# A transformer block on one core: where the first chunk of the MLP is projected, normalised and turned

## The reference, cut to what matters

```
# B = 2, N = 2048 tokens, H = 576, 16 heads of 36, MLP = 2304, all float32
mod = swish(c) @ w_mod + b_mod          # six vectors a batch: shift, scale, gate, twice
xn  = ln(x) * (1 + sc_msa) + sh_msa
q, k, v = split(xn @ w_qkv + b_qkv);  q = ln(q, g_q);  k = ln(k, g_k)    # per head
o   = softmax(q k^T / 6) v
x   = x + g_msa * (o @ w_proj + b_proj)
xn2 = ln(x) * (1 + sc_mlp) + sh_mlp
x   = x + g_mlp * (gelu_tanh(xn2 @ w1 + b1) @ w2 + b2)
```

## Time and profile before

| what | value |
|---|---|
| median of 3 runs | 2894.0 us (2893.54 to 2894.77) |
| the profiled execution | 2893.01 us, span 2891.1 us |
| PE busy | 2787.1 us, 96% |
| DVE, ACT, POOL busy | 1996.3, 1524.2, 689.4 us |
| last attention group | about 1709 to 1884 us of the span |
| between it and the first MLP product | 1883.94 to 1912.03 us |

### The profile page before, as it was taken

How to read it: one execution, slowest core, us unless ns; L and a number is a source line. 1 busy time by engine, 2 the same in 40 slices (tenths; PEclk the granted TensorE clock), 3 DMA queues, 4 the chain that set the end, 5 groups by cost and what they waited for, 6 DMA issues and landing times.

```text
span 2891.1 us, 43560 instructions
## 1 busy us (share of the span) xinstructions
PE 2787.1 (96%) x14764; PEld 1438.4 (50%) x14764; DVE 1996.3 (69%) x2677; ACT 1524.2 (53%) x2218; POOL 689.4 (24%) x502
## 2 busy tenths in 40 slices
PE   5579999999999999999999999989999999999999
PEld 1334444444444444444444444447575665757666
DVE  5668888888888888888888899954435344353421
ACT  2457777778887777777777777821211112121110
POOL 0143346642223333333333321010000000000000
PEclk9689999999999999999999999989999999999999
DMA  5142222222211122222223224140211202011000
GB/s 173 66 80 52 52 63 78 81 61 51 55 46 32 29 47 60 72 71 71 69 75 78 70 64 144 37 145 7 88 39 50 75 14 88 23 66 66 24 17 17
DMA packets 231121, 180.26 MB, mean 62 GB/s; under 512 B 148923, under 2 KB 176001, under 8 KB 230860
## 3 DMA queue, kind: packets, MB, share of 16 engines
q1 hardware_dynamic: 230694, 178.35, 22.4%
q10 hardware_dynamic: 296, 0.07, 0.0%
HBM read 98.77 MB, written 46.04 MB: 50 GB/s over the span
## 4 chain that ended last, share of the span: by engine, by line
PE 93%; DVE 2%; issue 1%; ACT 1%; POOL 1%; DVEq 0%; ACTq 0%; POOLq 0%
PE at_ps L1434 18%; PE at_ps L895 16%; PE at_ps L892 15%; PE at_ps L883 15%; PE at_ps L1458 15%; PE at_ps L911 10%; PE at_ps L949 1%; DVE at_plo L742 1%; PE at_ps L1424 1%; ACT at_aff L660 0%; PE at_ps L922 0%; ACT at_p L634 0%; POOL at_ssq L551 0%; PE at_ps L933 0%; ACT at_xy L608 0%
## 5 line engine op out<-in xcount | busy, mean ns | idle before, releaser
L742 DVE TENSOR_TENSOR at_plo<-at_p 128x1024 fp32r<-128x1024 f32 x1024 | 1267.0, 1258 | 199.2 <-ACT at_p L634 192.1
L634 ACT ACTIVATE at_p<-at_ps 128x1024 f32<-128x1024 f32 x1024 | 1047.0, 1025 | 406.9 <-PE at_ps L883 406.9
L895 PE MATMUL at_ps<-at_plo,at_vr 128*37 128x512 f32 x2048 | 1072.1, 591 | 0.0
L892 PE MATMUL at_ps<-at_p,at_v 128*73 128x512 bf16 x2048 | 796.3, 389 | 0.7 <-DVE at_plo L742 0.7
L1434 PE MATMUL at_ps<-ml_w2s,ml_hid 128*128 128x288 f16 x3456 | 428.1, 286 | 2.0 <-issue 2.0
L1458 PE MATMUL at_ps<-ml_xhi,ml_w 128*128 128x512 f16 x1296 | 399.2, 381 | 3.5 <-issue 3.5
L1434 PEld LDWEIGHTS at_ps<-ml_w2s,ml_hid 128*128 128x128 f16 x3456 | 338.0, 98 | 86.9 <-issue 2.5
L892 PEld LDWEIGHTS at_ps<-at_p,at_v 128*73 128x73 f16 x2048 | 232.7, 114 | 241.0 <-DVE at_plo L742 2.3
L537 POOL TENSOR_TENSOR at_tssq<-at_tssq,head_eps 128x8 f32<-128x8 f32 x112 | 124.0, 1107 | 924.3 <-DVE at_tssq L712 924.3
L895 PEld LDWEIGHTS at_ps<-at_plo,at_vr 128*37 128x37 f32 x2048 | 233.5, 114 | 222.5
L911 PE MATMUL at_ps<-wq,at_xhi 128*128 128x432 f16 x1008 | 297.6, 350 | 19.1 <-DVE at_txc L716 18.5
(11 more groups left out here) (150 smaller groups left out, 2313.6 us busy)
## 6 DMA issues: line engine op xcount, KB each, us to landing
head_sums<-at_oT SPq DMA_DIRECT2D x256, 72.0 KB
ml_held<-head_sums SPq DMA_DIRECT2D x64, 256.0 KB
at_xy<-in_L_cond_w SPq DMA_DIRECT2D x34, 288.0 KB
w_halves<-wq SPq DMA_DIRECT2D x68, 144.0 KB
at_xy<-in_x SPq DMA_DIRECT2D x32, 288.0 KB, 2.8
ml_x<-in_x SPq DMA_DIRECT2D x8, 1152.0 KB, 5.6
out<-ml_x SPq DMA_DIRECT2D x7, 1152.0 KB, 4.5
wm<-in_L_cond_w_mod SPq DMA_DIRECT2D x6, 1152.0 KB, 13.9
```

Source lines behind the costliest of these rows:

```text
L634: act.activation(p[:, s % NP, :], ps[:, 2 * (s % 2):2 * (s % 2) + 2, :].rearrange("p a n -> p (a n)"), ACT.Exp).then_inc(exp_done, 1)
L742: nc.vector.tensor_tensor(plo[:, s % NP, :], p[:, s % NP, :], high, ALU.subtract).then_inc(plo_ready, 1)
L892: nc.tensor.matmul(acc[0:VW, bass.ds((U % 2) * CH, CH)], v16[:, h % 2, 2 * s + a, 0:VW], high, start=(s == 0 and a == 0), stop=False, skip ...
L895: last = nc.tensor.matmul(acc[0:RW, bass.ds((U % 2) * CH, CH)], vr[:, h % 2, 2 * s + a, 0:RW], plo[:, s % NP, a * CH:(a + 1) * CH], start= ...
```

## The change

In the last attention group the PE loop over units is written out, and the work of chunk 0 gets places inside it.

- The five blocks of sums follow each other one unit apart (units 4 to 8, formerly two); the addition of the two parts moves from DVE to POOL; DVE multiplies in step 3, ACT casts in step 5, DVE subtracts in step 6.
- The projection of token tile i is made in unit 9+i: three pairs of matmuls in each of steps 2 and 3, two in each of steps 4 to 7, in banks 6 and 7. DVE multiplies by the gate in step 7; in unit 10+i it adds (step 0), makes moments (steps 1, 2) and the normal form (step 5).
- In unit 14 PE turns the five blocks (steps 0, 1, 3, 4, 6), ACT scales, shifts and casts (steps 1, 2, 4, 5, 7), DVE subtracts (steps 2, 3, 5, 6 and step 0 of unit 15).
- SP loads the gates' rows in unit 1 and w1 in unit 8. POOL's power of chunk 0 comes in units 10 to 13, and its addition of the second bias to the residual rows (L1242) may begin once the last normal form is made.
- After the group `up(0)` comes at once. SP's order after the group, and the places of chunk 1's additions and casts inside `up(0)`, are the same. DVE's reciprocal of the second denominators now comes before anything else that DVE does there.

```diff
+                if G == GROUPS - 1:
+                    rest.gpsimd_early(pool, u)
...
+                    if G == GROUPS - 1 and fixed:
+                        rest.tensor_early(pe, u, s)
...
+                    for u in range(UNITS):
+                        attend(G, u // NCH, u % NCH)
+                    continue
...
-    SUMS_AT, ADD_IN, MULTIPLY_IN, HIGH_IN, LOW_IN = ({u0 + 2 * k: k for k in range(KC)} for u0 in (4, 5, 6, 7, 7))
+    SUMS_AT, ADD_IN, MULTIPLY_IN, HIGH_IN, LOW_IN = ({u0 + k: k for k in range(KC)} for u0 in (3, 4, 4, 4, 4))
+    PROJECT_IN = {9 + i: i for i in range(TPC)}
+    PROJECT_AT = (None, None, (0, 3), (3, 6), (6, 8), (8, 10), (10, 12), (12, 14))
+    NORMAL_IN = {10 + i: i for i in range(TPC)}
+    TURN_IN = 14
+    TURN_AT, AFFINE_AT, LOW_X_AT = ({s: k for k, s in enumerate(at)} for at in ((0, 1, 3, 4, 6), (1, 2, 4, 5, 7), (2, 3, 5, 6)))
...
+    def early_pair(self):
+        return self.ps[:, 6:8, 0:HALF]
...
+            sp.dma_start(self.gates[:, :, :, :].rearrange("p b v n -> p (b v n)"), bcast(self.gates_dram, 0, P)).then_inc(self.gates_loaded, 16)
...
-        if u == 5:
+        if u == 8:
             self.load_w1(sp)
-        if u == 7:
-            sp.dma_start(self.gates[:, :, :, :].rearrange("p b v n -> p (b v n)"), bcast(self.gates_dram, 0, P)).then_inc(self.gates_loaded, 16)
...
+    def gpsimd_early(self, pool, u):
+        if u in self.ADD_IN:
+            k = self.ADD_IN[u]
+            pool.wait_ge(self.held_loaded[k % 2], 16 * self.so_far[k])
+            pool.tensor_tensor(self.total(k), self.total(k), self.slot[:, k % 2, 1, :], ALU.add).then_inc(self.added, 1)
+        if u in self.NORMAL_IN:
+            i = self.NORMAL_IN[u]
+            pool.wait_ge(self.first_mv, i + 1)
+            pool.tensor_tensor(self.rstd[:, 0, i:i + 1], self.mv[:, i, 1:2], self.keep.eps[:, 0:1], ALU.add).then_inc(self.first_var, 1)
+            pool.wait_ge(self.first_var, i + 1)
+            pool.tensor_tensor(self.rstd[:, 1, i:i + 1], self.rstd[:, 0, i:i + 1], self.keep.power[:, 0:1], ALU.pow).then_inc(self.first_rstd, 1)
...
-        if u in self.ADD_IN and s == 2:
-            self.add_o(dve, 0, self.ADD_IN[u])
-        if u in self.MULTIPLY_IN and s == 2:
+        if u in self.MULTIPLY_IN and s == 3:
             self.multiply_o(dve, 0, self.MULTIPLY_IN[u])
-        if u in self.LOW_IN and s == 5:
+        if u in self.LOW_IN and s == 6:
             self.low_o(dve, 0, self.LOW_IN[u])
+        if u == 9 and s == 1:
+            self.nc.vector.memset(self.xlo[KT:P, KF, :], 0.0).then_inc(self.xlo_zero, 1)
+            dve.wait_ge(self.gates_loaded, 16)
+            dve.wait_ge(self.x_loaded, 16)
+        if u in self.PROJECT_IN and s == 7:
+            i = self.PROJECT_IN[u]
+            self.gate_part(dve, i, i, self.early_pair, 0, 0)
+        if u in self.NORMAL_IN:
+            i = self.NORMAL_IN[u]
+            if s == 0:
+                self.add_part(dve, 0, i, i, self.x1_ready)
+            if s == 1:
+                dve.wait_ge(self.x1_ready, i + 1)
+                for h in range(2):
+                    last = self.nc.vector.bn_stats(self.stats[:, i, h, :], self.x1[:, i, h * HALF:(h + 1) * HALF])
+                last.then_inc(self.first_stats, 1)
+            if s == 2:
+                dve.wait_ge(self.first_stats, i + 1)
+                self.nc.vector.bn_aggr(self.mv[:, i, :], self.stats[:, i, :, :].rearrange("p a b -> p (a b)")).then_inc(self.first_mv, 1)
+            if s == 5:
+                dve.wait_ge(self.first_rstd, i + 1)
+                row = self.x1[:, i, :]
+                for c0, c1, at in ((0, H, 0), (KF * P, H, H)):
+                    last = self.nc.vector.tensor_scalar(self.tok[:, i, at:at + c1 - c0], row[:, c0:c1], self.mv[:, i, 0:1],
+                                                        self.rstd[:, 1, i:i + 1], ALU.subtract, ALU.mult)
+                if i == TPC - 1:
+                    last.then_inc(self.y_ready, 1)
+        if u == self.TURN_IN and s in self.LOW_X_AT:
+            self.low_x(dve, 0, self.LOW_X_AT[s])
+        if u == self.TURN_IN + 1 and s == 0:
+            self.low_x(dve, 0, KF)
...
-        nc.vector.memset(self.xlo[KT:P, KF, :], 0.0).then_inc(self.xlo_zero, 1)
-        dve.wait_ge(self.gates_loaded, 16)
-        first_project()
...
+    def tensor_early(self, pe, u, s):
+        if u in self.PROJECT_IN and self.PROJECT_AT[s]:
+            i, (n0, n1) = self.PROJECT_IN[u], self.PROJECT_AT[s]
+            ops = list(split_products(self.ohi, self.olo, self.wp, slice(i * P, (i + 1) * P), slice(0, H)))
+            if n0 == 0:
+                if i == 0:
+                    pe.wait_ge(self.olo_ready, KC)
+                    pe.wait_ge(self.wp_loaded, 16 * 7)
+                    pe.wait_ge(self.ends.t_yn, self.TILES + 1)
+                else:
+                    pe.wait_ge(self.pair_taken, i)
+            for n in range(n0, n1):
+                l, w = ops[n]
+                for half in range(2):
+                    last = self.nc.tensor.matmul(self.early_pair[:, half, :], l, w[:, half * HALF:(half + 1) * HALF],
+                                                 start=(n == 0), stop=(n == len(ops) - 1))
+            if n1 == len(ops):
+                last.then_inc(self.pair_ready, 1)
+        if u == self.TURN_IN and s in self.TURN_AT:
+            if s == 0:
+                pe.wait_ge(self.pair_taken, TPC)
+            self.turn_y(pe, 0, (self.TURN_AT[s],))
...
-                if J == 0 and i == 0:
-                    pe.wait_ge(self.wp_loaded, 16 * 7)
-                    pe.wait_ge(ends.exp_done, self.UNITS_DONE * STEPS + 2)
-                if J == 0 and i == 1:
+                if J == 1 and i == 1:
...
+                    pe.wait_ge(ends.exp_done, self.UNITS_DONE * STEPS + 2)
...
-        project(0, 0)
-        turn_y(0, range(KC))
```

More of the change, by code:

```diff
@@ L1227, in gpsimd @@
         for J in range(self.CHUNKS):
[L1228 to L1234, removed]
+            if J:
                 pool.wait_ge(self.mv_ready, J)
@@ L1247, in high_o, with affine @@
         act.copy(self.ohi[:, k, :], self.total(k)).then_inc(self.ohi_ready, 1)
+    def affine(self, act, J, k):
+        n = J * KC + k
+        act.wait_ge(self.xt_ready, n + 1)
+        act.wait_ge(self.xlo_ready, n + (0 if k else 1))
+        col = lambda v: self.keep.cols[:, J // NCH, v, k:k + 1]
+        act.activation(self.aff[:, k % 2, :], self.tr_bank(k), ACT.Identity, bias=col(2), scale=col(3)).then_inc(self.aff_ready, 1)
+        act.wait_ge(self.aff_ready, n + 1)
+        act.copy(self.xhi[:, k, :], self.aff[:, k % 2, :]).then_inc(self.xhi_ready, 1)
     def scalar_early(self, act, u, s):
-        if u in self.HIGH_IN and s == 0:
+        if u in self.HIGH_IN and s == 5:
             self.high_o(act, 0, self.HIGH_IN[u])
+        if u == self.TURN_IN and s in self.AFFINE_AT:
+            self.affine(act, 0, self.AFFINE_AT[s])
     def scalar(self, act):
[L1254 to L1262, removed]
         def gelu(J, f):
@@ L1269, in gelu @@
                            scale=1.0 / WS).then_inc(self.gelu_done, 1)
-        affine(0)
         act.wait_ge(self.b1_loaded, 16)
@@ L1279, in scalar @@
             if more:
-                affine(J + 1)
+                for k in range(KC):
+                    self.affine(act, J + 1, k)
     def add_o(self, dve, J, k):
@@ new lines, in vector_early, with gate_part @@
+        if u == self.TURN_IN and s in self.LOW_X_AT:
+            self.low_x(dve, 0, self.LOW_X_AT[s])
+        if u == self.TURN_IN + 1 and s == 0:
+            self.low_x(dve, 0, KF)
+    def gate_part(self, dve, i, r, pair, b, v):
+        dve.wait_ge(self.pair_ready, r + 1)
+        gate = self.gates[:, b, v, :].rearrange("p (h n) -> p h n", h=2)
+        self.nc.vector.tensor_tensor(self.part[:, i % 2, :].rearrange("p (h n) -> p h n", h=2), pair, gate, ALU.mult).then_inc(self.pair_taken, 1)
@@ new lines, in add_part, with low_x @@
+    def add_part(self, dve, J, i, r, after):
+        row = self.x1[:, (J % 2) * TPC + i, :]
+        dve.wait_ge(self.pair_taken, r + 1)
+        self.nc.vector.tensor_tensor(row, row, self.part[:, i % 2, :], ALU.add).then_inc(after, 1)
+    def low_x(self, dve, J, k):
+        rows = P if k < KF else KT
+        dve.wait_ge(self.xhi_ready, J * KC + k + 1)
+        self.nc.vector.tensor_tensor(self.xlo[0:rows, k, :], self.aff[0:rows, k % 2, :], self.xhi[0:rows, k, :], ALU.subtract).then_inc(self.xlo_ready, 1)
@@ L1316, in residual @@
         def residual(J, i, r, v, after):
[L1318 to L1323, removed]
+            self.gate_part(dve, i, r, self.pair(i), J // NCH, v)
+            self.add_part(dve, J, i, r, after)
         def project(J, r0):
@@ L1347, in project @@
             last.then_inc(self.y_ready, 1)
[L1349 to L1378, removed]
         def hidden(J, f):
@@ L1392, in down @@
                 if turn:
[L1393 to L1397 removed]
+                    for k in self.WITH_DOWN[i]:
```

(13 more changed lines are left out.)

8 lines of the change are left out of this document (5 added, 3 removed).

## The result

The kernel became slower by 0.32%: 2902.79 us (median of 7, 2900.54 to 2904.12) against 2893.54 (7 runs, 2891.69 to 2894.77) of the kernel before; the ratio is 1.0032, 95% interval 1.0021 to 1.0044. The forecast was 2901, range 2889 to 2907. The profiled execution took 2903.68 us, its span is 2901.8.

A forecast was written before the change was run, and what follows sets the result against it. PE was taken to bound attention. From attention's former end to the second projection, 16.1 + 3.6 + 15.1 + 16.5 + 39.3 + 2.7 = 93.3 us against 85.2; 8.1 us on the profiled 2893.0 gave 2901, range 2889 to 2907.

The forecast's parts named there:

- work moved into the group: Last attention group on PE: 112 projection matmuls at 13.8 us and 20 turns at 2.3 us, together 16.1 us.
- block 0 landed: First block of chunk 1's sums arrives 28.6 us after attention's end on PE, 6.6 us after being asked for.
- PE's stall: In `up(0)`: PE stops at 15.1 us after attention and goes on at 31.6, a new stall of 16.5 us.
- What bounds it, and the gap's worth: PE bounds attention; the gap before `up(0)`, which starts 28.1 us after attention, is the target; half clock costs 2.7 us.
- What is late next: Inside `up(0)`: chunk 1's sums, queued behind w2, come only 2.6 us earlier than before, so DVE, ACT and PE wait.
- five tiles of credit: In `up(0)`: with three gelus done PE can finish five feature tiles, until 15.1 us after attention, then stops.
- rows 9: Profile row: a small store issued behind w1 in unit 5 was waited for 10.5 us; used to expect queueing behind w2.
- Stalls in attention: Last attention group: 1.0 us in units 4 to 8, 0.6 in 13 and 14, 2.0 from ACT; sum 3.6 us.
- A: Rival after attention: the reciprocals' store overtakes w2, so PE stops only 4.9 us; 2889.5 us, chance 0.13.
- B: Rival in `up(0)`: the sums land before DVE asks, no new wait; 11.1 us less, 2882 us, chance 0.08.
- C: Rival: attention stretches; POOL blocks DVE for whole instructions, or ACT's unit 14 bursts cost twice; 2907 us, chance 0.11.
- D: Rival in `up(0)`: the wait comes, but PE's clock doesn't fall or the cast doesn't block gelu; 2898.5 us, chance 0.10.

The follow-up runs named there:

- the four runs on the order: The changed kernel with SP's order of w2, the reciprocals' store and chunk 1's sums altered in four ways: 2902.73, 2889.07, 2895.59 and 2904.24 us.
- e3_ask_later: The changed kernel, with DVE adding chunk 1's sums behind feature tiles 3, 6, 9, 12, 14 instead of 1, 4, 7, 10, 13: 2895.78 us.
- e1_sums_first: The changed kernel, with SP issuing the reciprocals' store and blocks 0 and 1 of chunk 1's sums before all of w2: 2902.73 us.
- e7_gates_after: `e5_halves_later`, with POOL's addition of the second bias to the residual rows held back until attention has ended: 2883.82 us.
- e11_half_w2: The changed kernel, with half of w2 ahead of the reciprocals' store and the other half behind block 4 of chunk 1's sums: 2895.59 us.
- e5_halves_later: `e3_ask_later`, with SP issuing blocks 0 and 1 before w2's first half and its second half behind block 4: 2884.54 us.
- e10_add_on_dve: `e7_gates_after`, with the five early additions of the sums moved from POOL back to DVE: 2882.51 us.

## Why the prediction was right

| step | forecast | measured |
|---|---|---|
| work moved into the group | 16.1 | 16.0 (units 9 to 12: 14.35 for 10.9; turns 0.44 a block) |
| stalls there | 3.6 | 4.9 |
| SP asks for the sums, after the last attention sum | 22 | 21.05 |
| block 0 landed | 28.6 | 29.0 |
| PE's stall | 16.5 | 16.46 |
| attention to second projection | 73.6 | 73.4 (1906.46 to 1979.84) |
| total (measured: 20.9 - 11.9) | +8.1 | +9.0 |

- *What bounds it, and the gap's worth.* Right: the gap of 28.1 us went, and the half clock came back behind the new stall.
- *What is late next.* Right in each link: the queue behind w2 (the four runs on the order), DVE's place (`e3_ask_later`, which moved ACT's cast along with it), ACT's cast in front of the fourth gelu (20.52 us of wait there), five tiles of credit. Two sizes were off and cancelled: the store landed 1 us earlier, and block 0 took 7.9 us from the first request and not 6.6.
- *The base.* I added 8.1 to the profiled execution and not to the median of 2894.0, which would have given 2902.1.
- *The control of rows 9.* A small store that waited 10.5 us behind w1 was the one row that told the chain's order, and it held: 14.05 us behind w2 here, about 1.7 in `e1_sums_first` with nothing ahead (issued at 1913.12, the sums asked for at 1914.85).
- *Stalls in attention.* The sum was near, 3.6 for 4.9, partly by luck, for the split was wrong. I gave ACT 2.0 in unit 14; PE waited 0.4 us for it in the kernel after, and the stall left in `e7_gates_after` is 1.3. I gave DVE 1.6; the other 3.6 or so are its. The mis-sized term is what POOL costs DVE. I multiplied POOL's lengths where DVE was idle by the 0.26 of the earlier trace rows, whose POOL lengths are those beside DVE: 3.1 us. The nine additions took 25.9 us for the 11.9 I had put, and lengthened DVE's instructions by 9.5. The Trainium skill ("SBUF — State Buffer", "Who interferes with whom") says that a DVE instruction with two SBUF inputs and a GpSimd instruction that reads SBUF exclude each other whole. The trace agrees with it: each of the nine additions held up one such DVE instruction, by most of an addition's length, and the 9.5 us are nearer to its 11.9 than to my 3.1.
- *Rivals.* A and B are refuted by the kernel after: the store landed behind w2, and DVE waited 20.00 us. Of C, most came on DVE (6.4 us more than I had put, where C has 8.8), but little reached PE, 1.3 where C has 6. D did not happen: the clock fell as forecast, and the cast held the gelu back.

## What to carry to other kernels

When work moves ahead into a free stretch, list what its successor asks for, and when each answer starts: a chain that starts at a fixed event (here the end of attention) doesn't move with it. A large load without a near reader belongs behind the small ones that have one, and the issuing engine's own time in a full queue counts as well. Read how long an operation takes from rows where its neighbour is busy, and look at single instructions beside it: a mean over a group hides that a few are held up whole.

## What the runs showed of the hardware

- An issue of a DMA can block the issuing engine: x took 0.44 us to issue in one run and 7.36 behind w2, w2 itself 3.60 and 9.04. The reciprocals' store took 7.26 us to issue behind all of w2, and 0.34 behind half of it (`e11_half_w2`).
- The clock may fall after a very short stop. Before the last chunk's product with w2 PE stands 2.0 us. In nine of the twelve traces the clock then stays full, in three it falls to 0.50 (1.2 GHz), and the end of the kernel is 1.67 us longer. Windows of 3 us there, in `e5_halves_later` and `e7_gates_after`:

```profile
2825.00:2828.00 3.00, 3.00 (x15) 1.82 (x13) 0.00 (x0) 0.00 (x0) 0.00 (x0) 0.50 0.00 0
```

```profile
2825.00:2828.00 3.00, 3.00 (x27) 2.38 (x26) 0.00 (x0) 0.00 (x0) 0.00 (x0) 1.00 0.00 0
```

From the second projection to the end all kernels need 921.9 us or 923.6 (`e1_sums_first`, `e5_halves_later` and `e10_add_on_dve` are of the second kind). That hides the 1.5 us that `e1_sums_first` had won, and is noise for any comparison of two traces at this size. Why the clock falls in some and not in others is not shown.
- POOL's addition of 576 columns took 1.40 us where DVE left it alone and 2.80 beside DVE's subtractions of two operands; in return, each addition lengthened one DVE instruction by 0.9 to 1.2 us, the others not.
